# Moving the clip to the head of a Runge-Kutta step and spreading a mixture-of-experts FFN over 43 stages of the next two blocks

## What is computed

```python
def _derivative(q, p, drive, coupling, bias):
    i_couple = jnp.tanh(q) @ coupling.T
    dq = q - q ** 3 / 3.0 - p + drive + i_couple + bias
    dp = EPSILON * (q + ALPHA - BETA * p)
    return (dq, dp)
# one step: four derivatives, each of the state that the one before gives, then
q_next = jnp.clip(q + DT / 6.0 * (dq1 + 2 * dq2 + 2 * dq3 + dq4), -CLAMP, CLAMP)
p_next = jnp.clip(p + DT / 6.0 * (dp1 + 2 * dp2 + 2 * dp3 + dp4), -CLAMP, CLAMP)
...
probs = jax.nn.softmax(x @ W_router.T); rw, sel = jax.lax.top_k(probs, 2)   # x: all q of the scan
shared_out = (_silu_and_mul(x @ Ws_gate_up) @ Ws_down) * jax.nn.sigmoid(x @ W_sgate.T)
sparse_out = sum over the 8 experts e of combine[:, e] * (_silu_and_mul(x @ We_gate_up[e]) @ We_down[e])
return input + shared_out + sparse_out
```

## Time and profile before

| | before |
|---|---|
| median of 3 runs | 815.58 us (815.22 to 816.0) |
| the profiled execution | 815.89 us, its span 814.0 us |
| TensorE matmuls | busy 691.9 us (85%), x12101 |
| TensorE weight loads | busy 602.1 us (74%) |
| VectorE | busy 728.3 us (89%), x4608 |
| ScalarE | busy 396.6 us (49%) |
| GpSimd | busy 177.5 us (22%), x372 |
| mean granted TensorE clock | 0.993 of full |
| chain that ended last, by engine | DVE 56%, issue 19%, PE 11%, POOL 5%, ACT 4% |

### The profile page before, as it was taken

How to read it: one execution, slowest core, us unless ns; L and a number is a source line. 1 busy time by engine, 2 the same in 40 slices (tenths; PEclk the granted TensorE clock), 3 DMA queues, 4 the chain that set the end, 5 groups by cost and what they waited for, 6 DMA issues and landing times.

```text
span 814.0 us, 34324 instructions
## 1 busy us (share of the span) xinstructions
PE 691.9 (85%) x12101; PEld 602.1 (74%) x12101; DVE 728.3 (89%) x4608; ACT 396.6 (49%) x2187; POOL 177.5 (22%) x372
## 2 busy tenths in 40 slices
PE   0114599999999999999999999999999999999998
PEld 0013488878888878778887878888787878888887
DVE  0698899999999999999999999999999999999972
ACT  4103355454645455454645455464545455454544
POOL 0000023132221213122221213122231213122233
PEclk9999999999999999999999999999999999999999
DMA  8400000000000000000000000000000000000000
GB/s 331 131 0 2 1 3 3 9 3 9 3 10 2 4 10 2 10 3 9 4 8 4 3 9 4 9 3 9 4 2 10 3 9 4 9 3 10 2 10 8
DMA packets 8493, 13.69 MB, mean 17 GB/s; under 512 B 1504, under 2 KB 7840, under 8 KB 8064
## 3 DMA queue, kind: packets, MB, share of 16 engines
q1 hardware_dynamic: 8320, 11.50, 4.1%
HBM read 9.40 MB, written 2.10 MB: 14 GB/s over the span
## 4 chain that ended last, share of the span: by engine, by line
DVE 56%; issue 19%; PE 11%; POOL 5%; ACT 4%; DMA 2%; DVEq 1%; SPq 1%; POOLq 0%; ACTq 0%
DVE force L625 8%; DVE hidden L694 7%; DVE cubic L602 6%; DVE th_lo L597 6%; POOL hidden L753 5%; PE down_ps L453 4%; DVE p_sum L556 4%; DVE q L638 3%; DVE q_raw L638 3%; DVE p_part L535 3%; DMA e_s<-in_e_base 2%; PE coup_ps L387 2%; DVE rest L629 2%; ACT th_hi L294 1%; PE coup_ps L394 1%
## 5 line engine op out<-in xcount | busy, mean ns | idle before, releaser
L439 PE MATMUL up_ps<-q_hi,w 128*128 128x128 f16 x2176 | 226.4, 220 | 0.7 <-POOL q_lo L725 0.7
L387 PE MATMUL coup_ps<-th_hi,c 128*128 128x16 f16 x4096 | 183.7, 171 | 49.4 <-ACT th_hi L294 43.3
L294 ACT ACTIVATE th_hi<-q 128x32 f16<-128x32 f32 x384 | 88.1, 229 | 279.0 <-DVE q L638 279.0
L387 PEld LDWEIGHTS coup_ps<-th_hi,c 128*128 128x128 f16 x4096 | 146.0, 97 | 101.4 <-ACT th_hi L294 73.5
L753 POOL TENSOR_TENSOR hidden<-hidden,comb_s 128x128 f32<-128x128 f32 x272 | 126.8, 468 | 322.4 <-PE coup_ps L394 314.5
L439 PE MATMUL up_ps<-q_lo,w 128*128 128x128 f16 x1088 | 197.1, 220 | 0.0
L439 PEld LDWEIGHTS up_ps<-q_hi,w 128*128 128x128 f16 x2176 | 175.0, 98 | 0.8 <-POOL q_lo L725 0.8
L394 PE MATMUL coup_ps<-th_lo,c 128*128 128x16 f16 x2048 | 132.2, 173 | 31.1 <-DVE th_lo L597 22.8
L453 PE MATMUL down_ps<-hidden,wd 128*128 128x128 f32 x1088 | 157.8, 285 | 0.0
L394 PEld LDWEIGHTS coup_ps<-th_lo,c 128*128 128x128 f16 x2048 | 85.7, 97 | 66.4 <-DVE th_lo L597 38.0
L453 PEld LDWEIGHTS down_ps<-hidden,wd 128*128 128x128 f32 x1088 | 133.3, 191 | 0.0
(11 more groups left out here) (83 smaller groups left out, 888.6 us busy)
## 6 DMA issues: line engine op xcount, KB each, us to landing
wf<-in_w_up SPq DMA_DIRECT2D x1, 4224.0 KB, 18.1
xs<-in_x SPq DMA_DIRECT2D x1, 2048.0 KB, 8.1
wd<-in_w_down SPq DMA_DIRECT2D x1, 2048.0 KB, 22.6
out<-out_s SPq DMA_DIRECT2D x16, 128.0 KB, 2.1
sel<-in_spread SPq DMA_DIRECT2D x1, 408.0 KB, 18.1
cf<-in_coupling SPq DMA_DIRECT2D x1, 256.0 KB, 2.6
ident<-in_identity SPq DMA_DIRECT2D x1, 64.0 KB, 2.1
wd<-in_w_down SPq DMA_DIRECT2D x1, 64.0 KB, 22.6
```

The lines of the kernel that those rows point to most:

```text
L294: nc.scalar.activation(th_hi[:], q[:], ACT.Tanh).then_inc(hi_ready, 1)
L387: nc.tensor.matmul(coup_ps[:, m * B:(m + 1) * B], c16[:, part, k, m * P:(m + 1) * P], th_hi[:, k, :], start=part == m == k == 0, stop=Fals ...
L439: last = nc.tensor.matmul(up_ps[j % 4][:, h * TOK:(h + 1) * TOK], w16[:, part, k, h, j * P:(j + 1) * P], q[:, k, :], start=n == 0, stop=n ...
```

## The change

The diff does six things.

- In k = 0 the clip is issued ahead of `rest1`.
- `rest2` moves from the end of k = 0 to the start of k = 1; `base3` moves to where `base4` stood, and `base4` behind `force`.
- The tables are new: up, silu, hide, spread, weigh, copy and down all start later, the weighing leaves the stages with k = 3, and the last four weighings and the last seven down products lie in stages 32 to 38, which are stages 0 to 6 of the block after the next.
- `ROUTE_AT` has the sum and the maximum of `expo` in stage 3, not 4; the steps behind the routing move by one stage; the transpose stands in stage 11.
- The two `finish_chunk` of stages 2 and 3 become one `finish` of twice the size in stage 42, that is stage 10.
- `ffn_stages` gives for each stage first the older block's part, then the younger's, on every engine.

```diff
-UP_AT = [st for st in range(3, 25) if st % 4 != 2]
-HIDE_AT = [s + 2 for s in UP_AT]
-SPREAD_AT = [12, 15, 18, 22, 26]
+HIDE_AT = [6, 9, 11, 13, 14, 15, 17, 18, 19, 21, 22, 23, 25, 26, 27, 29, 30]
+SILU_AT = [s - 1 for s in HIDE_AT]
+UP_AT = [s - 2 for s in HIDE_AT]
+TURN_AT = 11
+SPREAD_AT = [13, 17, 21, 25, 29]
-WEIGH_AT = list(range(13, 30))
-DOWN_AT = [14, 18, 18, 22, 22, 25, 26, 26, 27, 27, 28, 28, 29, 29, 30, 30, 31]
+WEIGH_AT = [14, 16, 17, 18, 20, 21, 22, 24, 25, 26, 28, 29, 30, 32, 33, 34, 36]
+DOWN_AT = [18, 18, 22, 22, 26, 26, 29, 30, 30, 31, 32, 33, 34, 35, 37, 37, 38]
+FINISH_AT = STAGES + 10
...
-ROUTE_AT = {1: (0, 1), 2: (2,), 4: (3,), 5: (4,), 6: (5,), 7: (6,)}
-FINISH_AT = [2, 3]
+ROUTE_AT = {1: (0, 1), 2: (2,), 3: (3,), 5: (4,), 6: (5,), 7: (6,)}
...
+        def ffn_stages(b, st):
+            return [(f, at) for f, at in ((b - 2, st + STAGES), (b - 1, st)) if 0 <= f < BLOCKS]
+        def tail_stages():
+            return [x for st in range(FINISH_AT + 1) for x in ffn_stages(BLOCKS, st)]
...
                 if k == 0:
                     if t:
-                        dve.wait_ge(p_clipped, t)
-                    nc.vector.tensor_tensor(rest[0][:], drive[:, t, 0], p_now[:], ALU.subtract
-                                            ).then_inc(rest1_ready, 1)
-                    if t:
                         dve.wait_ge(q_ready, n)
                         if i == 1 and b:
                             dve.wait_ge(q_split, 2 * b)
                         nc.vector.tensor_scalar(q, q_raw[:], CLAMP, -CLAMP, ALU.min, ALU.max).then_inc(q_clipped, 1)
+                        dve.wait_ge(p_clipped, t)
+                    nc.vector.tensor_tensor(rest[0][:], drive[:, t, 0], p_now[:], ALU.subtract
+                                            ).then_inc(rest1_ready, 1)
                 slot()
...
                 if k == 1:
+                    dve.wait_ge(based, t + 1)
+                    nc.vector.scalar_tensor_tensor(rest[1][:], q0_of(i), R2_Q1, base[:, 0, :].rearrange(
+                        "p (m b) -> p m b", m=KC), ALU.mult, ALU.add).then_inc(rested, 1)
                     update_p()
-                    nc.vector.tensor_tensor(base3[:].rearrange("p m b -> p (m b)"), base[:, 1, :],
-                                            q0_of(i), ALU.add).then_inc(based_q, 1)
...
                 nc.vector.tensor_tensor(force[:], rest[k][:], cubic[:], ALU.subtract).then_inc(forced, 1)
-                if k == 0:
-                    dve.wait_ge(based, t + 1)
-                    nc.vector.scalar_tensor_tensor(rest[1][:], q, R2_Q1, base[:, 0, :].rearrange(
-                        "p (m b) -> p m b", m=KC), ALU.mult, ALU.add).then_inc(rested, 1)
+                if k == 1:
+                    nc.vector.scalar_tensor_tensor(base4[:], q0_of(i), R4_Q1, base[:, 2, :].rearrange(
+                        "p (m b) -> p m b", m=KC), ALU.mult, ALU.add).then_inc(based_q, 1)
...
                 nc.vector.tensor_tensor(
-                    out_s[:, m, :].rearrange("p (t b) -> p t b", t=STEPS),
-                    down_ps[:, m * TOK:(m + 1) * TOK].rearrange("p (t b) -> p t b", t=STEPS),
-                    xs[:, bass.ts(f, STEPS), m, :], ALU.add).then_inc(out_ready, 1)
+                    out_s[:].rearrange("p m (t b) -> p m t b", t=STEPS),
+                    down_ps[:, 0:KC * TOK].rearrange("p (m t b) -> p m t b", m=KC, t=STEPS),
+                    xs[:, bass.ts(f, STEPS)].rearrange("p t m b -> p m t b"), ALU.add).then_inc(out_ready, 1)
```

More of the change, by code:

```diff
@@ L236, in blocks @@
             for b in range(BLOCKS):
-                block_of(b, b - 1 if b else None)
+                block_of(b)
+        def ffn_stages(b, st):
+            return [(f, at) for f, at in ((b - 2, st + STAGES), (b - 1, st)) if 0 <= f < BLOCKS]
+        def tail_stages():
+            return [x for st in range(FINISH_AT + 1) for x in ffn_stages(BLOCKS, st)]
         @block.sync
@@ L347, in ffn, with one_block @@
                                        ).then_inc(comb_copied, 1)
-            def one_block(b, f):
+            def one_block(b):
                 for st in range(STAGES):
                     tanh(b, st)
-                    if f is not None:
-                        if isinstance(f, int) and st == 0:
-                            act.wait_ge(setup_v, SETUP_V)
-                        ffn(f, st)
+                    if b == 1 and st == 0:
+                        act.wait_ge(setup_v, SETUP_V)
+                    for f, at in ffn_stages(b, st):
+                        ffn(f, at)
             blocks(one_block)
-            for st in range(STAGES):
-                ffn(BLOCKS - 1, st)
+            for f, at in tail_stages():
+                ffn(f, at)
         @block.tensor
@@ L457, in ffn, with one_block @@
                         last.then_inc(down_ready, 1)
-            def one_block(b, f):
+            def one_block(b):
                 for st in range(STAGES):
                     couple(b, st)
-                    if f is not None:
-                        if isinstance(f, int) and st == 0:
-                            pe.wait_ge(in_wd, 2 * 16)
-                            pe.wait_ge(setup_v, SETUP_V)
-                        ffn(f, st)
+                    if b == 1 and st == 0:
+                        pe.wait_ge(in_wd, 2 * 16)
+                        pe.wait_ge(setup_v, SETUP_V)
+                    for f, at in ffn_stages(b, st):
+                        ffn(f, at)
+                    if b:
                         for _ in range(WARM[st]):
@@ L606, in scan_stage @@
                 elif k == 1:
-                    nc.vector.scalar_tensor_tensor(base4[:], q0_of(i), R4_Q1, base[:, 2, :].rearrange(
-                        "p (m b) -> p m b", m=KC), ALU.mult, ALU.add).then_inc(based_q, 1)
+                    nc.vector.tensor_tensor(base3[:].rearrange("p m b -> p (m b)"), base[:, 1, :],
+                                            q0_of(i), ALU.add).then_inc(based_q, 1)
                 elif k == 2:
@@ L696, in ffn, with one_block @@
                                                        ).then_inc(hidden_ready, 1)
-                if f and st in FINISH_AT:
-                    finish_chunk(f - 1, FINISH_AT.index(st))
-            def one_block(b, f):
+                if st == FINISH_AT:
+                    finish(f)
+            def one_block(b):
                 for st in range(STAGES):
                     def slot(st=st):
-                        if f is not None:
-                            ffn(f, st)
+                        for f, at in ffn_stages(b, st):
+                            ffn(f, at)
                     scan_stage(b, st, slot)
@@ L710, in _ @@
                                     ).then_inc(q_clipped, 1)
-            for st in range(STAGES):
-                ffn(BLOCKS - 1, st)
-            for m in range(KC):
-                finish_chunk(BLOCKS - 1, m)
+            for f, at in tail_stages():
+                ffn(f, at)
         @block.gpsimd
@@ L737, in ffn @@
                                             ).then_inc(parted, 1)
[L738 removed]
+                if st == 9:
                     pool.wait_ge(parted, f * PARTS + 3)
```

29 lines of the change are left out of this document (14 added, 15 removed).

## The result

The changed kernel is slower. Four runs of it have a median of 825.79 us (822.98 to 827.63), four of the kernel before beside them 815.79 us (815.22 to 816.38): 1.012 of the time before, with a 95% interval of 1.0085 to 1.0154. The prediction was 810.5 us with 800 to 823 as its range; the sign is wrong and the time lies outside the range. The profiled execution took 824.33 us, its span is 822.2, where 809.0 was forecast.

What follows compares the result with a forecast made beforehand. The loop of tanh, remainder, coupling and q was taken to set the time. Blocks 2 to 15 -5.9 us, block 1 -1.3, block 0 -0.6, tail +2.8: -5.0 in all, span 809.0, forecast 810.5 us, range 800 to 823.

Steps and rivals of the forecast that it cites:

- rival 5: TensorE's clock falls at each stage 3 stall, doubling the next two stages' products: 1.9 us a block, 837 us; chance 0.05.
- Clip first: In k = 0 the earlier clip gains 0.09 us a stage, over 8 stages -0.72 us a block.
- Rivals 2 and 3: Clip in k = 0: brings nothing, 822 us, chance 0.10; or brings all, 0.16 a stage, 802 us, chance 0.13.
- `rest2` out of k = 0: Stages 16, 20, 24, 28 each lose the 0.35 us by which they are longer: -1.40 us a block.
- `base4`: In k = 1, between force and q, just ahead of the weighing's start: taken to cost zero.
- Expo: `total`, read in stage 3, waits for expo behind a weighing; stage 3 becomes 3.13 us, +1.80 per block.
- Logits behind a down tile: TensorE's down tile in stage 0 delays the logits' copy; stage 1 at about 1.96 us, +0.56 a block.
- Stages 7, 19, 23: Stage 7 loses its `hidden`, -0.26 us; stages 19 and 23 have two down tiles without the spread, -0.27 us together.
- Stage 5: Loses one `hidden`; ScalarE's pace takes over halfway, so half the gain: -0.13 us a block.
- Block 1: Its terms, with +1.40 us for expo as no weighing stands there, sum to -1.3 us.
- Block 0: Seven k = 0 stages gain 0.09 us each from the clip: -0.6 us.
- Tail: After the last block: three more up tiles, +2.0 us, and a transpose moved 0.8 to 0.9 by later expo; +2.8 us.

Runs made afterwards that it cites:

- e1: The changed kernel with 28 unread TensorE products added in stage 3, before the wait for `th_lo`: 814.96 us, 0.999 of the kernel before.
- e5: The kernel before with only the sum and maximum of expo moved from stage 4 to stage 3: 845.31 us, 1.0364 of before.
- e4: The kernel before with only the scan's part of the change (clip first, `rest2`, `base3` and `base4` moved), tables and finish as before: 790.71 us, 0.9692 of before.
- e6: e3 with TensorE doing the logits ahead of the older block's down tile in stage 0: 789.52 us, 0.9685 of the kernel before.
- e3: e2 with the weighings of tiles 15 and 16 moved to stages 36 and 37, tile 15's down product to 38: 790.55 us, 0.9695 of before.
- e2: The changed kernel with the sum and maximum of expo put back from stage 3 to stage 4: 792.82 us, 0.9718 of the kernel before.

## Why the prediction was wrong

The table sets the forecast's parts of the span against the profiled execution of the changed kernel and of e1, which is the same kernel with its clock kept in all blocks from 2 on but block 4 (us; "blocks 2 to 15" is 14 times the mean; what lies before the first q and the blocks 0 and 1 are from the timeline).

| part | before | forecast | after | e1 |
|---|---|---|---|---|
| up to the first q | 56.0 | 56.0 | 56.9 | 55.7 |
| block 0 | 41.8 | 41.2 | 41.6 | 41.6 |
| block 1 | 46.1 | 44.8 | 46.5 | 47.4 |
| blocks 2 to 15 | 643.7 | 637.8 | 648.4 | 639.3 |
| tail | 26.4 | 29.2 | 28.9 | 28.9 |
| span | 814.0 | 809.0 | 822.2 | 812.9 |

**The step that failed is what the sum puts down for TensorE's clock: nothing.** It stood outside the sum, as rival 5. Of the 13 us between forecast and result 9 lie in blocks 2 to 15 and go when only the clock is kept (648.4 to 639.3), and 1.2 more lie in block 1. I had the mechanism, at 0.05, and with it a time of 837 us. Three things were wrong with it.

- The argument against it was that block 0 holds 1.00 with TensorE busy for 46%. Block 0 doesn't. The trace's table of the clock starts at 103.20 us, in stage 3 of block 1, and the rows show 1.00 where it has no entry. The products tell what was granted. Below are six and eleven of the unread ones in block 1, issued ahead of that time, then six in a stretch recorded at 1.00 and eleven in one recorded at 0.50:

```profile
99.53 0.80 PE L468 MATMUL warm_ps<-c 128*128 128x128 f16 x6
...
101.97 1.33 PE L468 MATMUL warm_ps<-c 128*128 128x128 f16 x11
...
145.26 0.49 PE L468 MATMUL warm_ps<-c 128*128 128x128 f16 x6
...
147.62 1.33 PE L468 MATMUL warm_ps<-c 128*128 128x128 f16 x11
```

  Up to 102.99 us these products start 107 ns apart, as in the stretches recorded at 0.50, and from 103.50 on 56. In block 0 itself, which has only the coupling's products, these start 27 ns apart, as in those stretches, and not 25, as at 1.00. In all eleven traces the spacing changes where the table starts. So block 0 ran at the lower level, 1.2 GHz, through the whole of the earlier trace rows's first stretch: busy for 46%, TensorE never got the higher level there, and the stretch says nothing against the rival.
- The other half of the argument was that two stages around the stall are about as full as block 0. They are fuller: 1.32 and 1.38 of 3.13 and 1.38 make 60%, and the clock fell all the same. Block 0's waits come in each stage and are 0.7 to 0.85 us; here is one of 1.81 us at `th_lo`'s products, which the timeline of block 6 shows on both sides:

```profile
336.60 1.64 POOL L737 TENSOR_TENSOR expo<-e_s,shifted 128x8 f32<-128x8 f32 x1
...
338.34 0.16 DVE L669 TENSOR_REDUCE total<-expo 128x1 f32<-128x8 f32 x1 [1.90 <-POOL expo L737]
...
338.69 0.19 DVE L608 TENSOR_TENSOR th_lo<-th,th_hi 128x32 f16<-128x32 f32 x1
...
338.93 0.26 PE L404 MATMUL coup_ps<-th_lo,c 128*128 128x16 f16 x4 [1.81 <-DVE th_lo L608]
```

- The rows of before held more that spoke for the rival. Its mean granted clock of 0.993 isn't 1, though it counts the first 103 us as 1.00, and the half clock of the last stretch in the earlier trace rows is too short to make that. Its windows at two places, in blocks 2 and 4, which I hadn't looked at:

```profile
148.60:151.00 2.40, 2.40 (x44) 2.40 (x42) 2.22 (x17) 0.96 (x5) 0.95 (x1) 0.50 0.21 65
240.50:243.00 2.50, 2.50 (x43) 2.50 (x41) 2.38 (x20) 1.10 (x7) 1.25 (x1) 0.50 0.17 52
```

The kernel before loses its clock three times, in blocks 2, 4 and 10, each time in stage 2, with no wait of TensorE of over 0.32 us just ahead. I read them so: the kernel before is near losing it in these very stages, and a longer wait there takes it over. e5, which adds nothing but the wait, has 13 low stretches for 3; no run puts such a wait into other stages, so that the place matters isn't shown. With these rows it would have been the likeliest of the rivals. The Trainium skill (TensorE: Matmul & The Clock Gate, "HAM oscillation — how this bites in real kernels") was the other warning; the traces agree with it on the pattern, a wait in every round, though not that each one throttles: ten blocks of fourteen. The waits in that section's own case are for DMA and some 3 to 5 us long, so the 837 us that rival 5 draws from it for a wait of 1.8 us were my extension of it, not its figure; and block 0's rows, in which I said that it doesn't show, are at 1.2 GHz throughout.

The price in rival 5 was too high: 1.9 a block, in every block. What the runs showed is 1.0 us in block 6 (stages 4 to 6 take 5.00, in block 7 4.00) and 0.64 over all blocks from 2 to 15 (46.31 against e1's 45.67): the low clock covers parts of three stages, and in the first two the products still fit beside the scan's other work (1.38 and 1.41); only stage 6 is plainly longer (2.21). The 0.3 a stage for the coupling's own products was wrong as well: its eight and four take 0.38 and 0.27 us in block 0 and 0.36 and 0.26 at 1.00; they are late because they stand behind the slower tiles.

Term by term of the sum, as medians:

- *Clip first*, -0.72: right. 1.38 in the quiet k = 0 stages, `cubic` at 0.60. Rivals 2 and 3 are out.
- *`rest2` out of k = 0*, -1.40: right, 1.38 in all four. But only 0.25 of the 0.35 a stage is `rest2`'s: the other 0.10 is owed to the weighings' leaving the k = 3 stages, which I hadn't priced (e4 has 1.47 to 1.48 there without it). The total is right by luck, as the change does both.
- *`base4`*, taken as zero: right, 187 ns over all 128, and so was `rest2` in its new place at 192 ns. The group rows after:

```profile
L591 DVE SCALAR_TENSOR_TENSOR rest<-q_trace,base 128x32 f32<-128x32 f32 x128 | 24.5, 192 | 0.4
...
L639 DVE SCALAR_TENSOR_TENSOR base<-q_trace,base 128x32 f32<-128x32 f32 x128 | 23.9, 187 | 0.2 <-issue 0.2
```

  The Trainium skill (SBUF — State Buffer, "SBUF: two separate sides") holds here: the operation that starts first isn't lengthened (70 of the 128 `base4` start 0.06 to 0.14 ahead of a weighing and take 183 to 188 ns). e6 shows its other half, `rest2` at 0.58 us behind q_lo. It doesn't hold for expo: in 15 blocks of the kernel before, `th_lo`, `cubic` and `force` start 0.65 to 1.24 us into its 1.64 and take their usual 0.18 to 0.19.
- *Expo*, +1.80: right to 0.01; stage 3 is 3.13. It is the largest loss by far, and it buys next to nothing: stage 4 takes 1.38, and 1.45 in e3 with the sum in it.
- *Logits behind a down tile*, +0.56: 0.44 was measured (1.84), the mean 0.48.
- *Stages 7, 19, 23*: right, 1.39 and 1.32.
- *Stage 5*, -0.13: with its clock kept, in e1, it is 1.31: right there.
- *Missed: stage 15*, +0.13 a block (1.32 to 1.45), 1.8 us in all. In stage 14 GpSimd does the first weighing of the block after a pause, and it starts late. Stage 15 of block 7 begins at 401.01:

```profile
401.05 0.46 POOL L760 TENSOR_TENSOR hidden<-hidden,comb_s 128x128 f32<-128x128 f32 x1 [5.39 <-PE coup_ps L404]
...
401.18 0.37 DVE L567 SCALAR_TENSOR_TENSOR p_sum<-q,p_sum 128x32 f32<-128x32 f32 x1
```

  The weighing of stage 14 thus lies wholly in stage 15, where elsewhere it starts 0.07 ahead of q, and `p_sum`, with two inputs from SBUF, takes 0.37; `th_lo` stands behind it. The 5.39 in the weighing's row says how long GpSimd had stood still. Why it then starts some 0.35 late isn't settled; no run was made on it.
- *Block 1*: 1.7 above the forecast. 1.2 of it is the clock again: before, the products' spacing goes to 56 ns at 103.20 us, in stage 3, and in the changed kernel at 115.33, in stage 10, and stages 5, 8, 9 and 10 take 1.64, 1.71, 1.70 and 1.46. What puts this off isn't settled; it is so in e2 as well, without the wait. Stages 14 and 25 are 0.33 and 0.36 longer than the quiet ones, with the clock at 1.00. e1 is 2.6 above the forecast, with 1.4 of the filling's own in stage 3.
- *Block 0*: 0.4 above. Its seven k = 0 stages went from 1.47 to 1.38 as forecast, but stage 13 takes 1.67 for 1.31, since `force` starts 0.36 late there; why is open. *Tail*: 28.9 for 29.2, right.

With the clock kept, as in e1, the forecast is 3.9 us off in span (812.9 for 809.0), 2.3 of it the filling's own: within the range, though such a time is hardly better than before. "Faster" at 0.66 rested on the clock being safe, and a forecast gain of 5 us could bear no miss of 10.
